# One of sixteen row sets of each edge chunk fetched by TensorE instead of a gather (graph layer with expert feed-forward, one core)

## The reference

```
xl   = layernorm(x)                                   # x: 6250 nodes x 256
h_f, h_r = xl @ W_fwd.T, xl @ W_rev.T                 # 64 features each
m    = h_f[src] * attr[:, 0:1] + h_r[src] * attr[:, 1:2]          # 200000 edges, sorted by dst
s    = leaky_relu(m @ attn.T, 0.2)                    # 4 heads
p    = exp(s - max(s));  out[n, head] = sum_{dst = n} m * p[head] / sum_{dst = n} p[head]
x    = x + out                                        # 6250 x 256
y    = layernorm(x);  x = x + layernorm(y + top-2-of-16-experts(y)) * gamma + beta
```

## Time and profile before

| | us |
|---|---|
| median of 3 runs | 2696.86 (2696.54 to 2698.02) |
| the profiled execution, its own time | 2704.01 |
| its span in the profile | 2702.3 |
| GpSimd's first gather of the edges starts | 61.70 |
| GpSimd's last gather of the edges starts | 2037.38 |

### The profile page before, as it was taken

How to read it: one execution, slowest core, us unless ns; L and a number is a source line. 1 busy time by engine, 2 the same in 40 slices (tenths; PEclk the granted TensorE clock), 3 DMA queues, 4 the chain that set the end, 5 groups by cost and what they waited for, 6 DMA issues and landing times.

```text
span 2702.3 us, 30423 instructions
## 1 busy us (share of the span) xinstructions
PE 1121.3 (41%) x6713; PEld 1043.4 (39%) x6714; DVE 1280.0 (47%) x3334; ACT 353.5 (13%) x1023; POOL 1780.2 (66%) x1910
## 2 busy tenths in 40 slices
PE   7222322232322332232322322322325659999980
PEld 6222322232322332232322322322325648888870
DVE  6534434434434434434434334434336866666657
ACT  3000000000000000000000000000003534444435
POOL 3777777777777777777777777777772763333326
PEclk8666566666666566665666566666665569999995
DMA  6222222222222222222222222222221585665558
GB/s 191 57 56 54 56 55 56 55 56 54 56 55 56 55 56 54 56 55 56 55 56 54 56 57 54 56 55 56 54 57 43 174 258 189 205 198 187 196 169 266
DMA packets 162092, 249.05 MB, mean 92 GB/s; under 512 B 48422, under 2 KB 103783, under 8 KB 161796
## 3 DMA queue, kind: packets, MB, share of 16 engines
q0 software_dynamic: 59712, 134.70, 20.2%
q1 hardware_dynamic: 102340, 113.91, 13.6%
HBM read 210.65 MB, written 38.69 MB: 92 GB/s over the span
## 4 chain that ended last, share of the span: by engine, by line
POOL 34%; issue 25%; DVE 17%; DMA 9%; PE 9%; DVEq 5%; ACT 1%; POOLq 0%; SPq 0%; ACTq 0%
POOL rows L233 33%; DMA rows<-node_table,index 6%; PE p_win L742 4%; DVEq L1495 3%; DVE p_part L832 3%; DVE hot_ex L864 2%; DVE p_y L1718 1%; PE p_y L1663 1%; PE p_h L1653 1%; DVE second L1698 1%; DVE hid_t L1690 1%; DVE shared L824 1%; DVE back L1703 1%; DVE rows L829 1%; DMA out<-shared 1%
## 5 line engine op out<-in xcount | busy, mean ns | idle before, releaser
L233 POOL DMA_INDIRECT rows<-node_table,index x1563 | 1476.2, 944 | 544.5 <-issue 477.5
L742 PE MATMUL p_win<-hot_ex,msg 128*65 128x128 f32 x3136 | 570.1, 366 | 1404.1 <-DVE hot_ex L864 1404.1
L742 PEld LDWEIGHTS p_win<-hot_ex,msg 128*65 128x65 f32 x3136 | 548.2, 199 | 1425.8 <-issue 1425.8
L829 DVE TENSOR_TENSOR rows<-rows,p_attr 128x1088 f32<-128x1088 f32 x98 | 126.3, 1288 | 1089.7 <-DMA rows<-node_table,index 1089.7
L1504 POOL DMA_INDIRECT expert_rows<-ys,back x104 | 102.0, 981 | 271.3 <-DVE ys L1723 195.9
L789 ACT ACTIVATE p_ex<-score,neg_shift 128x64 f32<-128x64 f32 x98 | 31.1, 318 | 1620.5 <-DVE score L849 1620.5
L864 DVE TENSOR_TENSOR hot_ex<-hot,p_ex 128x2048 f32<-128x2048 f32 x98 | 223.1, 2277 | 0.0
L1653 PE MATMUL p_h<-xt,shared 128*128 128x128 f32 x1664 | 211.6, 281 | 6.2 <-ACT xt L1595 6.0
L1653 PEld LDWEIGHTS p_h<-xt,shared 128*128 128x128 f32 x1664 | 199.1, 194 | 31.3 <-ACT xt L1595 28.5
L1663 PE MATMUL p_y<-shared,hid_t 128*128 x832 | 198.8, 382 | 2.5 <-DVE hid_t L1690 2.0
L1663 PEld LDWEIGHTS p_y<-shared,hid_t 128*128 128x128 f32 x832 | 151.1, 192 | 19.7 <-issue 3.1
(11 more groups left out here) (251 smaller groups left out, 1153.4 us busy)
## 6 DMA issues: line engine op xcount, KB each, us to landing
shared<-in_w SPq DMA_DIRECT2D x120, 512.0 KB, 4.1
rows<-node_table,index POOLq DMA_INDIRECT x1563, 2.5
xs<-dispatched SPq DMA_DIRECT2D x104, 129.5 KB, 3.6
shared<-expert_rows SPq DMA_DIRECT2D x12, 896.0 KB, 8.2
token_rows<-in_x SPq DMA_DIRECT2D x7, 768.0 KB, 9.2
out<-shared SPq DMA_DIRECT2D x6, 896.0 KB, 8.0
node_table<-rows SPq DMA_DIRECT2D x7, 408.0 KB, 2.9
dispatched<-pad_row SPq DMA_DIRECT2D x17, 129.5 KB
```

Source lines behind the costliest of these rows:

```text
L233: pool.indirect_dma_start(out=rows[:, s, k, :], out_offset=None, in_=table, in_offset=bass.IndirectOffsetOnAxis(ap=index[:, s, k:k + 1], a ...
L742: last = pe.matmul(psum[0:MSG, u * HEADS * W:(u + 1) * HEADS * W], msg[:, k, :], weighted[:, k, :, :].rearrange("p h w -> p (h w)"), start ...
L829: dve.tensor_tensor(rows[:, s, :, 0:COLS], rows[:, s, :, 0:COLS], attr_p[:, 0, :].unsqueeze(2).broadcast_to([P, K, COLS]), ALU.mult)\
```

## The change

In chunks 2 to 95 the sixteenth row set (`KG` = 15) is no longer gathered. TensorE makes it: the table is kept in SBUF in three bf16 parts (high, middle, low; their sum is the float32 value), in the memory of x, `token_rows`. For the 128 sources of the set VectorE makes 17 matrices of 0 and 1 (`onehot`, bf16, 128x128 each) in two instructions, and TensorE multiplies them by the parts: one matrix serves up to three tiles of nodes (g, g+17, g+34), so a set takes 17 x 3 = 51 bf16 matmuls of 408 columns (272 in the last two groups). Which of the three thirds of the result is an edge's own is picked with the masks `third`, by one ScalarE and two VectorE instructions. All this is done one chunk ahead (`LEAD` = 1). The sources as float32 `key` come from DRAM, broadcast to all partitions, once for two chunks. Because x is overwritten, it is loaded a second time when the last set has been made. The buffers of the parts' working values lie over `attr_all`, so `attr` is loaded after the parts are ready, not behind x. `hot` becomes bf16, and `score` has one slot in place of two. In each of the ten parts of the table stage ScalarE makes the high and the middle part by copies, and GpSimd the two differences (for the last three parts, `LATE` = 7 on, VectorE does, ahead of line 602); a slot of `tab` can be copied into only when the first difference of four parts earlier is taken. Two more gathers stand first, the sixteenth sets of chunks 0 and 1, so 25 are issued before `prepared` is waited for. `coming(s, it, LEAD)` is the set of chunk c + 1, or nothing outside chunks 2 to 95.

```diff
+                def low(i):
+                    pool.wait_ge(s_part, mid_at[i])
+                    pool.wait_ge(s_init, rest_at[i])
+                    pool.tensor_tensor(part_of_parts(i, 2), rest_of(i), part_of_parts(i, 1), ALU.subtract)\
+                        .then_inc(s_init, 1)
+
+                for i in range(LATE):
+                    n = PARTS[i + 1] - PARTS[i]
+                    pool.wait_ge(s_part, high_at[i])
...
+                    pool.tensor_tensor(rest_of(i), tab[:, i % 4, 0:n, :], part_of_parts(i, 0),
+                                       ALU.subtract).then_inc(s_init, 1)
...
+                pool.wait_ge(s_init, parts_done)
+                pool.wait_ge(s_chain, tab_left)
+                for s in range(HOT):
+                    pool.wait_ge(index_ready[s], 16)
+                    gather(pool, s, [KG], early_rows)
                 for s in range(EARLY + 1):
-                    pool.wait_ge(index_ready[s], 16)
-                    gather(pool, s, range(K if s < EARLY else EARLY_SETS), gathered[s])
+                    gather(pool, s, range(KG if s < EARLY else EARLY_SETS), gathered[s])
...
+                def high(i):
+                    for copies, n in copied_part(i):
+                        act.wait_ge(copies, n)
+                    act.activation(parts[:, PARTS[i]:PARTS[i + 1], 0, :], tab[:, i % 4, 0:PARTS[i + 1] - PARTS[i], :],
+                                   ACT.Copy).then_inc(s_part, 1)
+
+                def middle(i):
...
+                    act.activation(part_of_parts(i, 1), rest_of(i), ACT.Copy).then_inc(s_part, 1)
...
-                sp.wait_ge(s_wp, 1)
-                sp.dma_start(attr_all[:, :, :], attr).then_inc(s_attr, 16)
...
+                sp.wait_ge(s_init, parts_done)
+                sp.wait_ge(s_chain, late_done)
+                sp.wait_ge(s_edge, 16)
+                sp.dma_start(attr_all[:, :, :], attr).then_inc(s_edge, 16)
...
+                for i in (LATE, LATE + 2, LATE + 1):
+                    late_rest(i)
+                for i in range(LATE, NPART):
+                    late_low(i)
                 dve.wait_ge(s_tab, triples)
                 dve.wait_ge(s_edge, 16)
                 link(dve.tensor_copy(dst_rel[:, :], dst_i[:, :]))
...
-                    after(sp, gathered[s], 16 * K * it)
+                    after(sp, gathered[s], 16 * KG * it)
                     sp.dma_start(index[:, s, :], src[c] if isinstance(c, int)
                                  else src[ds(c, 1)].rearrange("a p k -> (a p) k")).then_inc(index_ready[s], 16)
+                    if s == 0 and not whole(it):
+                        sp.wait_ge(hot_built, 2 * HOT * it)
+                        sp.dma_start(key[:, :, :], keys[ds(it * HOT, HOT), :].partition_broadcast(P))\
+                          .then_inc(key_ready, 16)
...
-                    sets = K_LAST if final(c) else K
+                    sets = K_LAST if final(c) else K if whole(it) else KG
...
+                def keep_first(c, f, s, it):
+
+                    act.wait_ge(hot_rows, f + 1)
+                    after(act, msg_ready, c - RING + 1)
+                    act.activation(rows[:, s, KG, :], p_hot[:, 0:ROW], ACT.Copy, scale=third[:, 0, ds(f, 1)])\
+                       .then_inc(hot_third, 1)
...
                 def step(c, s, it, loaded):
+                    if coming(s, it, LEAD):
+                        fetch(*coming(s, it, LEAD))
                     pe.wait_ge(msg_ready, c + 1)
                     pe.wait_ge(val_ready, c + 1)
...
+                def fetch(f, s, it):
+
+                    after(pe, hot_kept, 2 * f)
+                    for gr in ORDER:
+                        if gr in (0, ORDER[HALF]):
+                            pe.wait_ge(hot_built, 2 * (HOT + f) + 1 + (gr > 0))
+                        width = len(range(gr, NT, GP))
+                        for m in range(3):
+                            last = pe.matmul(p_hot[:, 0:width * ROW], onehot[:, gr, :],
+                                             parts[:, gr:NT:GP, m, :], start=(gr == 0 and m == 0),
+                                             stop=(gr == ORDER[-1] and m == 2))
+                    last.then_inc(hot_rows, 1)
...
                 def step(c, s, it, loaded):
-                    dve.wait_ge(gathered[s], arrived(c, it))
+                    if coming(s, it, LEAD):
+                        build_hot(*coming(s, it, LEAD))
+                    all_rows(dve, c, s, it)
                     dve.wait_ge(attr_ready, c + 1)
...
                     extra_windows(c, s, loaded[s])
+                    if coming(s, it, LEAD):
+                        keep_others(*coming(s, it, LEAD))
+
+                def build_hot(f, s, it):
+
+                    dve.wait_ge(key_ready, 16 * it)
+                    after(dve, hot_rows, f)
+                    for a, b in ((0, HALF), (HALF, GP)):
+                        dve.tensor_tensor(onehot[:, a:b, :],
+                                          key[:, s, :].unsqueeze(1).broadcast_to([P, b - a, P]),
+                                          group_p[:, a:b].unsqueeze(2).broadcast_to([P, b - a, P]), ALU.is_equal)\
+                           .then_inc(hot_built, 1)
+
+                def keep_others(f, s, it):
+
+                    dve.wait_ge(hot_third, f + 1)
+                    row = rows[:, s, KG, :]
+                    for m in range(1, 3):
+                        after(dve, hot_kept, 2 * f + m - 1)
+                        dve.scalar_tensor_tensor(out=row, in0=p_hot[:, m * ROW:(m + 1) * ROW],
+                                                 scalar=third[:, m, ds(f, 1)], in1=row, op0=ALU.mult, op1=ALU.add)\
+                           .then_inc(hot_kept, 1)
...
+            sp.wait_ge(g["hot_rows"], NF - HOT)
+            for i in range(NG):
+                v, n = reloaded(i)
+                sp.wait_ge(v, n - 16)
+                sp.dma_start(token_rows[:, i * U:(i + 1) * U, :],
+                             g["x"][i * U * P:(i + 1) * U * P, :].rearrange("(u p) d -> p u d", p=P)).then_inc(v, 16)
...
+                dve.wait_ge(*reloaded(i))
                 for u in range(*GROUPS[q]):
```

More of the change, by code:

```diff
@@ L58 @@
 UB = NU // 7
+HOT = 2
+NF = HOT * (NIT - 1)
+KG = K - 1
 K_LAST = -(-(EDGES - (NCH - 1) * CHUNK) // P)
+GP = -(-NT // 3)
+HALF = -(-GP // 2)
+ORDER = list(range(HALF)) + list(range(NT - 2 * GP, GP)) + list(range(HALF, NT - 2 * GP))
+LEAD = 1
 EXTRA = 8192
-assert UPC * HEADS * W <= 512 and K_LAST > EARLY_SETS and EARLY < RING
+assert HOT == RING and EARLY < RING and NF % 3 == 0 and HALF <= NT - 2 * GP and UPC * HEADS * W <= 512
+assert K_LAST > EARLY_SETS
 MAXWIN = NP // W
@@ L219, in stage_edges @@
         behind = esb("behind", [P, NU])
-        s_x = g["s_x"]
+        third = esb("third", [P, 3, NF])
+        key = esb("key", [P, HOT, P])
+        group_first = esb("group_first", [P, GP])
+        key_ready = esem("keys_loaded")
+        early_rows = esem("early_rows_gathered")
+        s_x, hot_rows, keys = (g[n] for n in ("s_x", "hot_rows", "keys"))
+        over_x = token_rows[:, :, :].rearrange("p t d -> p (t d)").bitcast(BF16)
+        parts = over_x[:, 0:NT * 3 * ROW].rearrange("p (t m r) -> p t m r", t=NT, m=3)
+        onehot = over_x[:, NT * 3 * ROW:NT * 3 * ROW + GP * P].rearrange("p (g e) -> p g e", g=GP)
+        assert NT * 3 * ROW + GP * P <= 2 * NT * D and 3 * ROW * 2 <= D * 4
         index = esb("index", [P, RING, K], I32)
@@ L317, in copied_part, with rest_of, part_of_parts @@
                 return copied(-(-PARTS[i + 1] // TRIPLE))
+            high_at, mid_at, rest_at, low_at = {}, {}, {}, {}
+            act_steps, pool_steps = 0, 12
+            for i in range(NPART + 2):
+                if i < NPART:
+                    act_steps += 1
+                    high_at[i] = act_steps
+                if i >= 2:
+                    act_steps += 1
+                    mid_at[i - 2] = act_steps
+            LATE = NPART - 3
+            for i in range(LATE + 1):
+                if i < LATE:
+                    pool_steps += 1
+                    rest_at[i] = pool_steps
+                if i >= 1:
+                    pool_steps += 1
+                    low_at[i - 1] = pool_steps
+            parts_done = pool_steps
+            late_rest_at = {LATE: 2, LATE + 2: 3, LATE + 1: 4}
+            late_low_at = {LATE: 5, LATE + 1: 6, LATE + 2: 7}
+            tab_left, late_done = 4, 7
+            def rest_of(i):
+                n = PARTS[i + 1] - PARTS[i]
+                return last_rest[:, 0:n, :] if i == NPART - 1 else rest[:, i % 2, 0:n, :]
+            def part_of_parts(i, m):
+                return parts[:, PARTS[i]:PARTS[i + 1], m, :]
             def rows_of(dram, i):
@@ L356, in _ @@
                           allow_small_or_imprecise_dtypes=True).then_inc(s_ident, 1)
+                pool.iota(group_first[:, :], pattern=[[P, GP]], base=0, channel_multiplier=1,
```

(31 more changed lines are left out.)

105 lines of the change are left out of this document (92 added, 13 removed).

## The result

Four runs of the changed kernel gave 2558.6 to 2563.17 us, median 2563.1; four of the kernel before on the same chip 2693.62 to 2698.02, median 2696.7. The ratio is 0.9497, 95% interval 0.9485 to 0.9508: 133.6 us faster.

What follows compares the result with a forecast made beforehand. GpSimd's gathers were taken as the bound: 2704.0 - 118.9 (94 gathers) + 1 (table stage) + 1.5 (shift) + 0.5 (reload of x) = 2588.1 us, or 2581 us from the median 2696.86; range 2570 to 2612 us.

Steps and rivals of the forecast that it cites:

- the price of a removed gather: Edge stage: each gather removed from GpSimd saves 1.2646 us, so 94 of them save 118.9 us.
- the stall: Early edge stage: GpSimd waits for the first score after 25 gathers, 1.1 us, from 0 to 6, taken as +1.5 us.
- What bounds the kernel: Edge stage: GpSimd's gathers set the time, as long as no other engine's work nears 18.97 us a chunk.
- The table stage: Ahead of the edge stage: added copies and differences move the first gather from 61.70 to 62.7 us, +1 us.
- rival 1: Ahead of the edge stage: part-making is more exposed and `attr` late, +20 us there, 2601 us in all; chance 0.15.
- The shift: Softmax shift: `attr` loads later, the first score comes at about 95.4 us and GpSimd needs it at 94.3, +1.5 us.
- In the chunk: Edge loop: added VectorE, ScalarE, SyncE and TensorE work stays hidden beside GpSimd's gathers, 0 us.
- The clock gate: TensorE in the edge loop: idle time may halve its clock; forecast took sets at 8.3 to 9 us, near full clock.
- My room of 13.1 us: TensorE per chunk: 18.97 us less 5.3 for window sums and about 0.6 for hand-overs is free for a set.
- rival 2: Edge loop: TensorE becomes the bound from 13.1 us a set; at half clock 16.7 us, +216 us, 2913 us; chance 0.08.
- The reload of x: End of edge stage: second load of x is hidden, but last chunks' rows may come 0 to 3 us late, +0.5 us.
- 3 and 4: Edge loop: saving partly lost in the chunk, 2640 us, chance 0.05; no change, key loads holding back index loads, 0.02.

Runs made afterwards that it cites:

- a16_nohot: Changed kernel with its table stage, gather order and reload of x, but no TensorE sets and all sixteen sets gathered: 2703.46 us, ratio 1.0021 to the kernel before.
- b17: Kernel before with one gather more in each of chunks 2 to 95, into a tile nobody reads: 2791.55 us, ratio 1.0336.
- b15: Kernel before with the sixteenth gather of chunks 2 to 95 left out and nothing in its place: 2573.7 us, ratio 0.9535.
- a15_nohot: Changed kernel without TensorE's sets, fifteen gathers a chunk, the sixteenth rows left stale: 2577.01 us, ratio 0.955 to the kernel before.
- a_fetch15: Changed kernel with 24 of the 51 matmuls of each TensorE set issued once more in front: 2562.19 us, ratio 0.9491 to the kernel before.
- a_fetch2: Changed kernel with all 51 matmuls of each TensorE set issued twice: 2745.95 us, ratio 1.0173 to the kernel before.
- b_split: Kernel before with GpSimd's wait for the sums moved one gather later in the chunk, nothing left out: 2699.6 us, ratio 0.9997.
- b_pad: Kernel before with a GpSimd memset of 300 columns between the 11th and 12th gather of each chunk: 2719.93 us, ratio 1.0078.
- b_pad0: Kernel before with a GpSimd memset of 8 columns between the 11th and 12th gather of each chunk: 2699.17 us, ratio 1.0.
- a_fetch17: Changed kernel with 36 of the 51 matmuls of each TensorE set issued once more in front: 2562.48 us, ratio 0.9495 to the kernel before.

## Why the prediction was right, and where it failed

**The step that failed** is the price of a removed gather, and in it the sentence "All in all a gather costs 1976.6 / 1563 = 1.2646 us". I had seen the pauses, and averaged them over the gathers, 0.017 us each, as if a shorter row of gathers met fewer of them in proportion: 94 x 0.017 = 1.6 us of the -118.9. They did not shrink in proportion; they went altogether, -24.2 us by the two traces. The 94 gathers themselves are worth 94 x 1.248 = 117.3 us, as forecast. I wrote "about once in seven chunks", and did not ask what seven chunks are: one look at each of the 13 would have shown them exactly 112 gathers apart, and so tied to a number that the change alters. I could still not have known that 15 a chunk meet none; but a rival "the pauses go" at 2581 - 22.6 = 2558 us would have belonged to the range, and 2563.1 would have lain in it.

The account of the miss, by the two profiled executions: pauses -22.6 beyond what the price held, first gather +0.6, the stall -1.5, the end -1.6: -25.1 us. But the profiled execution of before took 7.3 us more than the median of its runs and that of after did not, so by medians the miss is -17.7: forecast -115.9, measured -133.6. The small terms are better taken from a16_nohot, which has all that the change adds outside the chunks: +5.9 us, where I had +1, +1.5 and +0.5. So by medians the pauses are -22.6 and the terms outside the chunks +2.9, together -19.7; the 2 us left are within what the medians of the kernel before differ by from chip to chip (2696.7 to 2699.87). Two terms were thus off, and the smaller one hid a part of the larger.

**What bounds the kernel**: right. GpSimd's gathers set the period before and after; b17 and b15 show it in both directions, about 1.25 us for one gather beside the pauses.

**The table stage** (+1 us, rival 1 at +20): the first gather is 1.6 us later by the two profiled executions, some 3 us by the means over all traces. VectorE's one wait of 5.35 us became five of 1.5 to 3.4 us, one of them on a subtraction of GpSimd; and the subtractions of 816 columns take 1.72 us each, inside the 0.72 to 2.30 that I had as bounds. GpSimd's last one ends at 60.21 us, and the last three parts' differences on VectorE from 60.15 to 64.45 us; then, on VectorE too, the reduction over `attr`, the shift and the first score:

```profile
58.49 1.72 POOL L449 TENSOR_TENSOR token_rows<-attr_all,token_rows 128x816 bf16<-128x816 f32 x1
```

```profile
60.15 2.12 DVE L737 TENSOR_TENSOR attr_all<-rows,token_rows 128x816 f32<-128x816 f32 x3
62.20 2.25 DVE L745 TENSOR_TENSOR token_rows<-attr_all,token_rows 128x816 bf16<-128x816 f32 x3
...
71.51 1.79 DVE L761 TENSOR_REDUCE ten<-attr_all 128x1 f32<-128x1568 f32 x1 [2.67 <-DMA attr_all<-in_attr]
...
90.10 0.16 DVE L818 COPY neg_shift<-p_tab 128x1 f32<-128x1 f32 x1 [0.68 <-PE p_tab L632]
...
94.76 0.22 DVE L1066 SCALAR_TENSOR_TENSOR score<-raw 128x64 f32<-128x64 f32 x1
```

**The shift** (+1.5 us): the chain came as worked out, `attr` issued at 64.60 (forecast 65.7), `neg_shift` at 90.3 (91.5), the first score at 94.98 (95.4). The gather that waits for it is number 25 from 0, at 95.91 without any stall, so the term is 0.

**In the chunk** (0 us): VectorE's matrices 2.48 us (2.55), the two that keep the result 0.35 us each (0.3); the wait for rows 5.4 to 6.6 us (6.8 of room). TensorE's set 8.62 us at a clock of 1.00 (8.3 to 9). b15, a15_nohot and a_fetch15 each bear out that none of it reaches the period.

**The clock gate.** I held against the change that the sums would begin slow after idle time (the Trainium skill, TensorE: Matmul & The Clock Gate, "Why this matters for your kernels"). The trace agrees: 5.2 us of idle time, then 0.50. What I did not draw from it is the other side of the same rule: a busier TensorE gets its sums at the full clock. My room of 13.1 us was 1.9 us too small: 1.6 for the sums (3.7 and not 5.3), 0.6 for hand-overs (in a_fetch2 sets and sums follow each other without a gap but for 0.45 us now and then), less 0.25 for the period (18.72 and not 18.97). That changed nothing at 8.62 us a set but overrated rival 2; its "16.7 us at half clock" never came, as all sets ran at the full clock: the mean of the 4794 matmuls is 329 ns, and that of the 9588 in a_fetch2 too.

**The reload of x** (+0.5 us): issued from 1867.54 to 1882.4, first used at 1922.66; the rows of chunks near the end came late once (VectorE waited 13.99 us for them at 1889.38), and from the last gather to the end it is 663.9 us, no longer than the 664.9 of before (659.0 to 662.5 in the five other kernels with the old table stage and 104 expert tiles).

**Rivals.** 1: measured at +1.6 to +3 of its +20 (+5.9 with all that stands outside the chunks). 2: the mechanism is real, as a_fetch2 shows, but begins between 14.5 and 17.1 us a set, worked out at 15.0. 3 and 4: no sign of either; line 1046 repeats every 18.66 us, and GpSimd waits for no index load.

**Open.** What the pause itself is: GpSimd's engine shows nothing in it, no wait of the kernel stands at its place (b_split), no code is loaded in the stage, and what ties it to the chunk was not found out. The Trainium skill (DMA: Bandwidth & Descriptors, "Terms") says that descriptors of DMAs issued from GpSimd are written to rings in SBUF; something that goes by count could hang on such a ring, but no row or run here shows it. The rows show pauses every 112 gathers for 14 and 16 a chunk and none for 15 and 17, and no more; even against odd was not tested. Not tried: a second set from TensorE in every other chunk. It would need 1.5 x 8.62 + 3.7 = 16.6 us of TensorE a chunk, and the period would be 14.5 x 1.248 = 18.1, so by these numbers there is room for some 47 x 1.248 = 59 us more. That is an estimate in the mean of two chunks: the one with two sets would need 17.2 + 3.7 = 20.9 us, and VectorE's part is left out.

## What to carry to other kernels

When a stage's time is "so many instructions by a mean", take the mean apart first: list the distances between the instructions, and where a few are much longer, note their ordinal numbers. If their spacing is a whole number of chunks (here 7), a change of the count per turn may move or remove all of them, and the range must hold both. And before a TensorE budget is drawn from a burst that began on half clock, recompute it with that burst at full clock: what is put into the idle time ahead of it can give a part back (here 2.0 of 5.7 us).

## What the runs showed of the hardware that was not expected

- A row of indirect gathers on GpSimd, 1.248 us apart, has a pause of 1.8 to 2.0 us more once in 112 gathers, when the chunks of the loop hold 14 or 16 of them (11 to 13 pauses, 22 to 26 us in all), and none with 15 or 17. It keeps its place by count when a chunk becomes 0.22 us longer (b_pad), when a wait is moved (b_split), and when the table stage ahead is another (a16_nohot, though its first pause is missing).
- A memset of 8 columns between two gathers costs nothing (b_pad0: ratio 1.0), since it fits into the 0.30 us that GpSimd is idle ahead of a gather; one of 300 columns, 0.37 us long, costs 0.22 us.
- 32 window sums in float32 take 5.0 to 6.7 us after 3.4 to 5.5 us of idle time on TensorE (the changed kernel), 5.4 us after 2.2 us (a_fetch15), and 3.7 us after 1.1 us or less (a_fetch17).
